# Groups of four with a wait for landing in the indirect DMAs of two routed feed-forward stages (eight-stage transformer block kernel, one core)

## Chip, core and metric

One core of a Trainium2 chip runs the whole program in one launch. The metric is the device time of that launch in microseconds (us); lower is better. Engines are called by their names in the profile: PE (TensorE), DVE (VectorE), ACT (ScalarE), POOL (GpSimd) and SP (the engine that issues the plain DMAs; SPq is its queue).

## What is computed

The reference adds eight residual blocks to x (4 sequences of 512 tokens, 128 features): an attention-like mixing block and a feed-forward block in turn, four times. The change touches the feed-forward blocks of the kernel's stages "1" and "3", in which each token goes to 2 of 8 experts (stage 1) or to 1 of 8 (stage 3):

```python
# stage 1 (L0_ffn), on the layer norm of x
global_idx, weights = _route(tokens, uzman_embeddings, onbellek_durumu)   # 2 of 8 experts, softmax weights
h = gelu(einsum('nd,edh->enh', tokens, W1) + b1[:, None, :])               # 128 -> 512
out_all = einsum('enh,ehd->end', h, W2) + b2[:, None, :]                   # 512 -> 128
out = sum(weights[..., None] * out_all[global_idx, arange(N)[:, None]], axis=1)
# stage 3 (L1_ffn), on the layer norm of x
one_hot = one_hot(argmax(xf @ Wg + bg, axis=-1), e)
h = gelu(einsum('td,edh->eth', xf, W1), approximate=True)
out = einsum('etd,te->td', einsum('eth,ehd->etd', h, W2), one_hot)
...
x = x + _L0_ffn_ref(_layernorm(x)); x = x + _L1_xcond_ref(...); x = x + _L1_ffn_ref(_layernorm(x)); ...
```

## The kernel before

Two streams of work, c0 and c1, each carry two of the four sequences (1024 tokens) through stages 1 to 5; their instructions share all engines. Stage 6 follows behind a barrier, with all four sequences apart.

A routed stage (generator `routed`, lines 1053 to 1187) does the following for each stream. The gates choose experts, and `rank` (DVE, L2811 at its end) gives each token a slot in a table in DRAM, in which every block of 128 rows belongs to one expert: 23 blocks in stage 1, 15 in stage 3. POOL then scatters the normed tokens to their slots in `zslots`, one indirect DMA of 128 rows of 512 bytes each (`zs`, L3059): 16 of them per stream in stage 1 (8 tiles of tokens times 2 experts), 8 in stage 3. When all have landed, SP fetches four blocks at a time back (`zl`, L1585). PE transposes them (`zbt`, L1827) and multiplies each block by its expert's first weights (`re1`, L1836; DVE copies these weights to a fixed place, L2781), ACT applies the gelu (L2311 in stage 1, L2308 in stage 3), and PE multiplies by the second weights (`re2`, L1846). DVE copies the result out of PSUM (L2820), and SP stores four blocks at a time in `yslots` (`ysd`, L1590). When all of them are stored, POOL gathers each token's rows back (`yg`, L3065), again 16 DMAs per stream in stage 1 and 8 in stage 3, and DVE adds them to x (`ya`, L2832 in stage 1, L2827 in stage 3), one half of the stream's tokens (k = 0, 1) at a time. In stage 1, small products with the experts' second bias run beside the scatter (`br1`: PE L1858, ACT L2295; `br2`: PE L1867, DVE L2675).

Every engine runs its own list of instructions in order. What stands where in these lists is decided when the program is built: the streams are generators that ask a planner (`Plan.merge`) for time on a chain of engines, with an estimated cost in us for each step, and the planner gives the next place to the stream whose step it expects to start first, with biases and a random term from a table per stage (`ORDER`). An expected cost therefore also sets the order on all engines. The planner counts 1.27 us for each indirect DMA on POOL (engine "G").

PE's completion is signalled by one semaphore (`T`, s_pe0 in the order rows), DVE's, ACT's and POOL's likewise; a DMA adds 16 to a semaphore of its own when it has landed, for instance `zs0` for the scatters of c0, `yg0_0` and `yg0_1` for the two halves of its gathers. `D(name).now()` is the value that such a semaphore has when everything that was issued on it up to this place has landed. In the trace's rows, a wait whose end the profile lays to nobody is called "remote".

Of the kernel before, what the change touches and what calls it, by code (L numbers as in the profile page):

```python
# [210 lines left out]
class Plan:  # L211
# [24 lines left out]
    def emit(self, *step):  # L236
        self.order.append(step)
# [92 lines left out]
def build(nc, d, out):  # L330
    ctx = ExitStack()
    with ctx:
        def sb(name, shape, dt=F32):
            return ctx.enter_context(nc.sbuf_tensor(name, shape, dt))[tuple(slice(None) for _ in shape)]


        T, A, V, G = (Sem(nc, ctx, n) for n in ("pe", "act", "dve", "pool"))
        chan = {}

        def D(name):  # L340
            if name not in chan:
                chan[name] = Sem(nc, ctx, name, 16)
            return chan[name]
# [53 lines left out]
        for i in range(2):  # L397
# [3 lines left out]
            n = f"c{i}"  # L401
            m = sb(n + "m", [128, 6144])
# [52 lines left out]
        for c in cos:  # L455
# [8 lines left out]
            for name, top, nk in (("1", 2, 23), ("3", 1, 15)):  # L464
                r = Co()
# [76 lines left out]
        for e in six:  # L542
            f, o = Co(), [4960 * (e.i // 2)]
# [67 lines left out]
        def uid():  # L611
            ids[0] += 1
            return ids[0]
# [34 lines left out]
        def do(name, *args, chain, after):  # L648
            _, t = yield Want(chain, after=after)
            emit(name, *args)  # L650
            return t[-1]
# [177 lines left out]
        def chain(c):  # L829

            for name, run in (("1", lambda: routed(c, "1")), ("2", lambda: both(stage2, c)),
                              ("3", lambda: routed(c, "3")), ("4", lambda: both(stage4, c)),
                              ("5", lambda: ahead(stage5, experts5, c))):
                while name == "2" and len(zero) < 5:
# [218 lines left out]
        def routed(c, name):  # L1053

            r, n = c.route[name], uid()
# [4 lines left out]
            def add(k, t):  # L1060
                yield from do("ya", r, n, k, chain=[("V", .7 if name == "3" else 2.4)], after=t)
                added.append(k)
# [54 lines left out]
            def scatter():  # L1117
                t = tp
                for j in range(8):
                    for m in range(r.top):  # L1120
                        t = yield from do("zs", r, n, j, m, chain=[("G", 1.27)], after=t)
                slots.append(t + 2.0)

            def fetch():
                while not slots:
                    yield
                for h in range(nb):
# [7 lines left out]
                    have[h] = zt, t[1]  # L1135

            plan.spawn(scatter(), c)
            plan.spawn(weights(), c)
            plan.spawn(fetch(), c)
# [7 lines left out]
            for i in range(nk + 1):  # L1147
# [12 lines left out]
                if i >= 1:  # L1160
                    k = i - 1
# [8 lines left out]
                    else:  # L1170
                        _, t = yield Want([("T", .95)], [], th)
# [8 lines left out]
            t = max(stored)  # L1180
            for k in range(2):
                for j in range(4):
                    for m in range(r.top):
                        t = yield from do("yg", r, n, 4 * k + j, m, chain=[("G", 1.27)], after=t)
                plan.spawn(add(k, t + 2.0), c)
            while len(added) < 2:
                yield
# [1862 lines left out]
        def gpsimd(e):  # L3050
            w = Waits(e)
# [4 lines left out]
            def zs(r, n, j, m):  # L3056
                w.wait_ge(*D("st_z").at("z"))
                w.wait_ge(*V.at(("pos", n)))
                e.indirect_dma_start(out=r.ZD, out_offset=bass.IndirectOffsetOnAxis(ap=r.pos[m][:, j:j + 1], axis=0), in_=r.Z[:, j, :],  # L3059
                                     in_offset=None).then_inc(*D(f"zs{r.i}")(("zs", n)))  # L3060

            def yg(r, n, j, m):
                for q in range(2):
                    w.wait_ge(*D(f"ys{r.i}_{q}").at(("ys", n)))
                e.indirect_dma_start(out=r.G[m][:, j, :], out_offset=None, in_=r.YD,  # L3065
                                     in_offset=bass.IndirectOffsetOnAxis(ap=r.pos[m][:, j:j + 1], axis=0)
                                     ).then_inc(*D(f"yg{r.i}_{j // 4}")(("yg", n, j // 4)))
# [84 lines left out]
            def ybg(c, m, vec):  # L3152
                w.wait_ge(*G.now())
                e.tensor_tensor(c.y, c.y, bc4(vec), ALU.add).then_inc(*G(("yb", m)))

            run(dict(zs=zs, yg=yg, fence=fence, pre=pre, ln=ln, cx0=cx0, pre2=pre2, lnb=lnb, s0base=s0base, en=en, s1g=s1g, sa=sa, bar=bar,
                     lng=lng, rp=rp, rps=rps, ybg=ybg))

# [187 lines left out]
```

## Time and profile before

| | us |
|---|---|
| runs of before (device time) | 4064.53, 4055.73, 6461.04; median 4064.53 |
| the profiled execution's own time | 4054.01 |
| span of that execution (first to last instruction) | 4052.2 |
| PE busy in the span | 3451.3 (85%) |
| DVE, ACT, POOL busy | 2498.2 (62%), 2258.0 (56%), 1420.3 (35%) |
| mean granted TensorE clock, share of full | 0.939 |
| indirect DMAs on POOL, stages 1 and 3 | 48 scatters (L3059), 48 gathers (L3065) |

All numbers of the trace are from one profiled execution, and times within it count from its first instruction. Stage 1 lies at about 200 to 440 us, stage 2 up to about 1060, stage 3 at about 1033 to 1173, and stages 4 and 5 follow up to about 2115, where the barrier before stage 6 stands. In a timeline row, the bracket at the end is the time that the engine sat idle before the row and who ended that wait.

### The profile page before, as it was taken

How to read it: one execution, taken by the hardware profiler on the slowest of the kernel's cores; microseconds unless marked ns; L12 is line 12 of the kernel's file. 1: busy time of each engine (PE TensorE's matmuls, PEld its weight loads, DVE VectorE, ACT ScalarE, POOL GpSimd, SP SyncE). 2: the span in 40 equal slices, each digit the busy share in tenths (PEclk: the TensorE clock that was granted, in tenths of full speed). 3: DMA queues.
4: the chain of work that ended last, by engine and by line, in shares of the span. 5: the costliest groups of instructions: out<-in, count | busy, mean ns of one | idle time of the engine just before them, and what ended most of it. 6: DMA issues, size and time to landing. Idle time of an engine off the chain costs nothing.

```text
span 4052.2 us, 56657 instructions
## 1 busy us (share of the span) xinstructions
PE 3451.3 (85%) x21861; PEld 1520.2 (38%) x21861; DVE 2498.2 (62%) x4786; ACT 2258.0 (56%) x3258; POOL 1420.3 (35%) x1419
## 2 busy tenths in 40 slices
PE   5637799899789988998886888999999999988987
PEld 3437333333543344334552233333333333333334
DVE  6642543543455435543658878778777778777754
ACT  4514455455245464545322766767777777667773
POOL 4541443443344402440004144343442433433321
PEclk8758899999899999999996999999999999999987
DMA  3011100000210010001112001111111110110100
GB/s 121 10 53 55 57 17 12 17 17 12 74 55 17 22 38 12 16 22 57 33 29 57 25 25 49 44 33 41 44 46 27 44 49 25 50 42 25 42 12 16
DMA packets 139215, 146.07 MB, mean 36 GB/s; under 512 B 37241, under 2 KB 120649, under 8 KB 137238
## 3 DMA queue, kind: packets, MB, share of 16 engines
q1 hardware_dynamic: 135876, 136.16, 11.5%
q0 software_dynamic: 3072, 6.30, 0.5%
q8 instruction: 174, 2.85, 0.3%
q14 instruction: 93, 0.76, 0.1%
HBM read 69.20 MB, written 12.59 MB: 20 GB/s over the span
## 4 chain that ended last, share of the span: by engine, by line
PE 57%; DVE 23%; ACT 9%; POOL 5%; issue 3%; another core or an unknown queue 2%; DMA 1%; SPq 1%; POOLq 0%; DVEq 0%; ACTq 0%
PE ps L1978 7%; PE ps L1962 6%; PE ps L2173 5%; DVE c1sm L2950 4%; DVE c0sm L2950 4%; PE ps L2090 3%; PE ps L2159 3%; ACT wA L2422 2%; PE ps L1903 2%; PE ps L2010 2%; PE ps L2117 2%; PE ps L2217 2%; PE ps L2209 2%; PE ps L1836 2%; POOL c1m L3131 2%
## 5 line engine op out<-in xcount | busy, mean ns | idle before, releaser
L2422 ACT ACTIVATE wA<-ps 128x1024 f32<-128x1024 f32 (+1 forms) x576 | 580.3, 1022 | 190.2 <-PE ps L2159 185.8
L2950 DVE TENSOR_REDUCE c1sm<-ps 128x2 f32<-128x1024 f32 x384 | 454.7, 1219 | 103.8 <-PE ps L2117 102.2
L2950 DVE TENSOR_REDUCE c0sm<-ps 128x2 f32<-128x1024 f32 x384 | 453.6, 1219 | 92.0 <-PE ps L2117 90.4
L2725 DVE TENSOR_REDUCE c1sm<-ps 128x2 f32<-128x1024 f32 x128 | 154.8, 1222 | 194.0 <-PE ps L1927 191.8
L2725 DVE TENSOR_REDUCE c0sm<-ps 128x2 f32<-128x1024 f32 x128 | 154.5, 1222 | 168.3 <-PE ps L1927 165.8
L2422 ACT ACTIVATE c0m<-ps 128x1024 f32<-128x1024 f32 (+1 forms) x195 | 199.4, 1023 | 63.4 <-PE ps L2159 62.0
L2422 ACT ACTIVATE wB<-ps 128x1024 f32<-128x1024 f32 (+1 forms) x189 | 193.1, 1022 | 56.8 <-PE ps L2159 55.4
L3080 POOL TENSOR_SCALAR c1sm<-c1sm 128x4 f32<-128x4 f32 x40 | 7.9, 196 | 536.0 <-DVE c1sm L2494 535.8
L2159 PE MATMUL ps<-c0ar 64*128 64x512 bf16 (+1 forms) x864 | 165.3, 385 | 28.1 <-DVE c1sm L2950 12.1
L1962 PE MATMUL ps<-c0ar 64*128 64x512 f32 (+1 forms) x640 | 178.3, 635 | 11.4 <-ACT c0ar L2345 7.4
L3080 POOL TENSOR_SCALAR c0sm<-c0sm 128x4 f32<-128x4 f32 x40 | 7.9, 196 | 512.6 <-DVE c0sm L2494 427.2
L2173 PE MATMUL ps<-wA,c1m 128*9 128x512 f32 (+1 forms) x932 | 182.1, 599 | 1.5 <-ACT wB L2422 0.9
L2159 PE MATMUL ps<-c1ar 64*128 64x512 bf16 (+1 forms) x864 | 163.9, 387 | 21.3 <-DVE c0sm L2950 11.8
L3124 POOL TENSOR_TENSOR c0ar<-c0ar 128x1024 f32<-128x1024 f32 x52 | 123.0, 2366 | 165.2 <-ACT c0ar L2352 132.0
L1962 PE MATMUL ps<-c1ar 64*128 64x512 f32 (+1 forms) x640 | 174.2, 621 | 5.1 <-ACT c1ar L2345 2.7
L2117 PE MATMUL ps<-c1ar 62*128 62x512 bf16 x768 | 151.1, 392 | 23.0 <-DVE c1sm L2950 6.9
L2117 PE MATMUL ps<-c0ar 62*128 62x512 bf16 x768 | 149.5, 390 | 17.8 <-DVE c0sm L2950 9.0
L3137 POOL TENSOR_TENSOR c0m<-c0m 128x512 f32<-128x512 f32 (+1 forms) x78 | 96.7, 1240 | 183.8 <-DVE c0m L2939 162.1
L3124 POOL TENSOR_TENSOR c1ar<-c1ar 128x1024 f32<-128x1024 f32 x52 | 123.6, 2377 | 104.9 <-ACT c1ar L2352 91.4
L2352 ACT ACTIVATE c0ar<-ps 128x1024 f32<-128x1024 f32 (+1 forms) x96 | 98.3, 1024 | 108.6 <-PE ps L1965 108.2
L2352 ACT ACTIVATE c1ar<-ps 128x1024 f32<-128x1024 f32 (+1 forms) x96 | 98.3, 1024 | 108.5 <-PE ps L1965 106.9
L2939 DVE TENSOR_TENSOR c0m<-ps,CST 128x1024 f32<-128x1024 f32 x72 | 88.2, 1225 | 61.0 <-PE ps L2090 60.9
(979 smaller groups left out, 8290.2 us busy)
## 6 DMA issues: line engine op xcount, KB each, us to landing
c0ar<-c0m SPq DMA_DIRECT2D x216, 128.0 KB, 2.4
c1ar<-c0m SPq DMA_DIRECT2D x216, 128.0 KB, 2.4
c0m<-rscr SPq DMA_DIRECT2D x96, 128.0 KB, 3.0
c1m<-rscr SPq DMA_DIRECT2D x96, 128.0 KB
wA<-in_x SPq DMA_DIRECT2D x1, 4112.0 KB, 21.9
wA<-in_x SPq DMA_DIRECT2D x1, 4096.0 KB, 13.0
wA<-in_lay SPq DMA_DIRECT2D x3, 1346.0 KB, 5.9
wB<-in_lay SPq DMA_DIRECT2D x3, 1346.0 KB, 5.9
```

What stands on the lines that cost most here:

```text
L1962: e.matmul(j4(u.ap, h, 512)[0:n, :], c.KT[s][r, o:o + n], c.QT[s][r, :], start=True, stop=False)
L1978: x = e.matmul(acc.ap[64 - 64 * h:128 - 64 * h, :], c.VV[g % 2][0:n, i, 64 * h:64 * h + 64], P.ap[0:n, h, :], start=first, stop=end, skip_ ...
L2090: i = e.matmul(U.ap[:, 512 * k:512 * k + ncol], j4(ww, k), src, start=True, stop=True)
L2117: i = e.matmul(j4(u.ap, p, 512), c.QS[r, s, 128 * j:128 * j + 128], c.KS[r, s, :], start=True, stop=True)
L2159: i = e.matmul(j4(u.ap, p, 512)[0:n, :], K, c.QS[r, s, :], start=True, stop=True)
L2173: x = e.matmul(acc.ap[32 * i:32 * i + (9 if g % 2 else 18), :], vv, Ps[i // 2].ap[0:n, i % 2, :], start=first, stop=end, skip_group_check= ...
L2352: e.activation(P.ap[0:n, :, :], u.ap[0:n, :].rearrange("p (h q) -> p h q", h=2), ACT.Exp, scale=0.125).then_inc(*A(("P", n0, g, i), free=[u]))
L2422: e.activation(P.ap[0:n, :, :], u.ap[0:n, :].rearrange("p (a q) -> p a q", a=2), ACT.Exp, scale=S8).then_inc(*A(("P8", n0, s, k), free=[u]))
L2725: e.tensor_reduce(c.sm[:, 2 * (g % 2), 2 * j:2 * j + 2], u.ap.rearrange("p (h k) -> p h k", h=2)[:, :, 0:n], AX, ALU.max, negate=True).the ...
L2950: e.tensor_reduce(c.mneg[:, j, :, s // 4, s % 4], u.ap.rearrange("p (a k) -> p a k", a=2), AX, ALU.max, negate=True).then_inc(*V(free=[u]))
L3124: e.tensor_tensor(S.ap, P0.ap if P0 else S.ap, P.ap, ALU.add).then_inc(*G(("S", n0, g), free=[P0, P] if P0 else [P]))
L3137: e.tensor_tensor(o[:, 0:ncol], o[:, 0:ncol], o[:, 512:512 + ncol], ALU.add).then_inc(*G(("rp", n)))
```

## The change

POOL waits, before every fourth indirect DMA after the first of a stream's scatter or gather, until those issued before on the same semaphore have landed. That makes 3 waits for each run of 16 and 1 for each run of 8: 12 in stage 1 and 4 in stage 3. The planner's expected cost of the waiting DMA rises from 1.27 to 3.47 us, so that the order on all engines is planned anew from that place to the barrier before stage 6.

```diff
@@ routed, scatter() @@
                     for m in range(r.top):
-                        t = yield from do("zs", r, n, j, m, chain=[("G", 1.27)], after=t)
+                        rest = 2.2 if (r.top * j + m) % 4 == 0 and (j or m) else 0.0
+                        t = yield from do("zs", r, n, j, m, chain=[("G", 1.27 + rest)], after=t)
@@ routed, the gathers @@
                     for m in range(r.top):
-                        t = yield from do("yg", r, n, 4 * k + j, m, chain=[("G", 1.27)], after=t)
+                        rest = 2.2 if (r.top * j + m) % 4 == 0 and (k or j or m) else 0.0
+                        t = yield from do("yg", r, n, 4 * k + j, m, chain=[("G", 1.27 + rest)], after=t)
@@ gpsimd @@
             def zs(r, n, j, m):
                 w.wait_ge(*D("st_z").at("z"))
                 w.wait_ge(*V.at(("pos", n)))
+                if (r.top * j + m) % 4 == 0 and (j or m):
+                    w.wait_ge(*D(f"zs{r.i}").now())
                 e.indirect_dma_start(out=r.ZD, ...)
             def yg(r, n, j, m):
                 for q in range(2):
                     w.wait_ge(*D(f"ys{r.i}_{q}").at(("ys", n)))
+                if (r.top * j + m) % 4 == 0 and (j or m):
+                    w.wait_ge(*D(f"yg{r.i}_{(r.top * j + m - 1) // r.top // 4}").now())
                 e.indirect_dma_start(out=r.G[m][:, j, :], ...)
```

On POOL, at the scatters of stage 1, the list before was this (zslots is the table in DRAM, c0ar and c1ar hold the normed tokens; s_zs00 is the semaphore on which the scatters of c0 land):

```order
L3059 DMA zslots<-c0ar 2944x128 [waits s_dve0,s_st_z0]
L3059 DMA zslots<-c0ar 2944x128 x15
L3059 DMA zslots<-c1ar 2944x128 [waits s_dve0]
L3059 DMA zslots<-c1ar 2944x128 x15
L3065 DMA c0ar<-yslots,c0ar 128x128 [waits s_ys0_10,s_ys0_00]
```

and it is now this, with the lines shifted by the added ones:

```order
L3063 DMA zslots<-c0ar 2944x128 [waits s_dve0,s_st_z0]
L3063 DMA zslots<-c0ar 2944x128 x3
L3063 DMA zslots<-c0ar 2944x128 [waits s_zs00]
L3063 DMA zslots<-c0ar 2944x128 x3
L3063 DMA zslots<-c0ar 2944x128 [waits s_zs00]
L3063 DMA zslots<-c0ar 2944x128 x3
L3063 DMA zslots<-c0ar 2944x128 [waits s_zs00]
L3063 DMA zslots<-c0ar 2944x128 x3
L3063 DMA zslots<-c1ar 2944x128 [waits s_dve0]
L3063 DMA zslots<-c1ar 2944x128 x3
L3063 DMA zslots<-c1ar 2944x128 [waits s_zs10]
L3063 DMA zslots<-c1ar 2944x128 x3
```

The scatters of c1 still stand behind all of those of c0; nothing else has come between them. On SP, the DMAs after these scatters were (zl fetches from zslots, ysd stores to yslots):

```order
L1585 DMA c0ar<-zslots 128x4x128 [waits s_zs00]
L1585 DMA c0ar<-zslots 128x4x128
L1585 DMA c0ar<-zslots 128x4x128 [waits s_pe0]
L1590 DMA yslots<-c0m 128x4x128 [waits s_dve0]
L1585 DMA c0ar<-zslots 128x4x128 [waits s_pe0]
L1585 DMA c1ar<-zslots 128x4x128 [waits s_zs10]
L1585 DMA c0ar<-zslots 128x4x128 [waits s_pe0]
```

and are now

```order
L1587 DMA c0ar<-zslots 128x4x128 [waits s_zs00]
L1587 DMA c0ar<-zslots 128x4x128
L1587 DMA c0ar<-zslots 128x4x128 [waits s_pe0] x2
L1592 DMA yslots<-c0m 128x4x128 [waits s_dve0]
L1587 DMA c0ar<-zslots 128x4x128 [waits s_pe0]
L1592 DMA yslots<-c0m 128x4x128 [waits s_dve0]
L1587 DMA c1ar<-zslots 128x4x128 [waits s_zs10]
```

The first fetch of c1 has moved behind the fifth fetch and the second store of c0, and PE's first transposes and experts of c1 have moved behind more experts of c0 with it. The third place is POOL's list at the gathers of c1 in stage 1; before it was

```order
L3080 TENSOR_SCALAR c0ve<-c0mv 128x4 [waits s_pool0,s_dve0]
L3082 TENSOR_TENSOR c0rs<-c0ve,MH 128x4 [waits s_pool0]
L3080 TENSOR_SCALAR c0ve<-c0mv 128x4 [waits s_pool0,s_dve0]
L3082 TENSOR_TENSOR c0rs<-c0ve,MH 128x4 [waits s_pool0]
L3065 DMA c1ar<-yslots,c1ar 128x128 [waits s_ys1_10,s_ys1_00]
L3065 DMA c1ar<-yslots,c1ar 128x128 x15
L3124 TENSOR_TENSOR c0ar<-c0m 128x1024 [waits s_pool0,s_act0]
```

and now it is

```order
L3086 TENSOR_SCALAR c0ve<-c0mv 128x4 [waits s_pool0,s_dve0]
L3088 TENSOR_TENSOR c0rs<-c0ve,MH 128x4 [waits s_pool0]
L3071 DMA c1ar<-yslots,c1ar 128x128 [waits s_ys1_10,s_ys1_00]
L3086 TENSOR_SCALAR c0ve<-c0mv 128x4 [waits s_pool0,s_dve0]
L3088 TENSOR_TENSOR c0rs<-c0ve,MH 128x4 [waits s_pool0]
L3071 DMA c1ar<-yslots,c1ar 128x128 x3
L3071 DMA c1ar<-yslots,c1ar 128x128 [waits s_yg1_00]
```

The second layer norm of c0 in stage 2 (TENSOR_SCALAR and TENSOR_TENSOR on c0ve and c0rs) now stands behind the first gather of c1, and with it behind the stores of c1's last experts.

## Rows read from the trace of the kernel before

**Rows 1.** Stretches: its length, each engine's busy us (instructions), PE clock, DMA share, GB/s.

```profile
core 0: us, PE busy (x) PEld busy (x) DVE busy (x) ACT busy (x) POOL busy (x), PEclk, DMA share, GB/s
240.00:500.00 260.00, 169.91 (x1148) 129.20 (x1148) 94.85 (x228) 97.21 (x263) 86.59 (x80) 0.80 0.18 56
500.00:1040.00 540.00, 522.88 (x2955) 204.02 (x2953) 245.42 (x366) 271.22 (x437) 214.62 (x99) 0.99 0.06 16
1040.00:1200.00 160.00, 115.50 (x785) 87.69 (x784) 71.14 (x188) 50.13 (x79) 54.34 (x50) 0.86 0.22 74
```

**Rows 2.** Timeline of POOL, stage 1 scatters: start, length, operation, [idle before and its end].

```profile
238.01 1.24 POOL L3059 DMA_INDIRECT zslots<-c0ar  x1 [11.69 <-DVE c1ar L2616]
...
257.41 1.03 POOL L3059 DMA_INDIRECT zslots<-c0ar  x1 [0.30 <-issue]
258.75 1.16 POOL L3059 DMA_INDIRECT zslots<-c1ar  x1 [0.30 <-issue]
...
277.92 0.96 POOL L3059 DMA_INDIRECT zslots<-c1ar  x1 [0.30 <-issue]
```

**Rows 3.** Timeline of the other engines beside the scatters of c1, stage 1.

```profile
259.73 28.39 SPq L1585 DMA_DIRECT2D c0ar<-zslots  x3
...
259.98 2.07 PE L1867 MATMUL ps<-EQS,c1m 8*128 8x128 f32 x8 [2.73 <-issue]
...
261.98 1.01 PE L1858 MATMUL ps<-CST,c1ar 128*8 128x128 f32 x4
279.64 0.69 DVE L2675 TENSOR_TENSOR X<-X,ps 128x512 f32<-128x512 f32 x1 [20.57 <-remote]
283.16 0.59 ACT L2295 ACTIVATE c1m<-ps 8x512 f32<-8x512 f32 x1 [23.23 <-remote]
...
283.80 2.07 PE L1867 MATMUL ps<-EQS,c1m 8*128 8x128 f32 x8 [20.80 <-ACT c1m L2295]
...
286.62 1.11 PE L1827 MATMUL ps<-CST,c0ar 128*128 128x128 f32 x4 [0.76 <-issue]
```

**Rows 4.** Timeline beside the gathers of c0 (POOL from 364.04), stage 1.

```profile
372.53 1.14 ACT L2311 ACTIVATE c1m<-ps,c1ar 128x128 f32<-128x128 f32 x4 [5.32 <-remote]
...
375.69 1.91 PE L1836 MATMUL ps<-c1m,c1ar 128*128 128x128 f32 x8
...
382.87 0.94 POOL L3065 DMA_INDIRECT c0ar<-yslots,c0ar  x1 [0.30 <-issue]
...
386.65 2.18 ACT L2311 ACTIVATE c1m<-ps,c1ar 128x128 f32<-128x128 f32 x8 [12.07 <-remote]
387.95 2.07 PE L1846 MATMUL ps<-wA,c1m 128*128 x8 [10.34 <-ACT c1m L2311]
```

**Rows 5.** Timeline at the last gather of c1 in stage 1 and beside it.

```profile
427.26 0.31 PE L1939 MATMUL ps<-c0ar 64*128 64x77 bf16 x8 [1.52 <-issue]
...
433.69 0.95 POOL L3065 DMA_INDIRECT c1ar<-yslots,c1ar  x1 [0.31 <-issue]
...
436.56 0.81 DVE L2732 TENSOR_REDUCE ps<-ps 128x8 f32<-128x616 f32 x1 [5.69 <-remote]
```

**Rows 6.** Timeline behind the scatters of c0 in stage 3: fetch and first transpose.

```profile
1057.58 4.56 SPq L1585 DMA_DIRECT2D c0ar<-zslots  x3
1060.68 1.06 PE L1827 MATMUL ps<-CST,c0ar 128*128 128x128 f32 x4
```

**Rows 7.** Timeline at the scatters of c1 in stage 3 and beside them.

```profile
1080.14 1.06 POOL L3059 DMA_INDIRECT zslots<-c1ar  x1 [14.26 <-DVE c1ar L2811]
...
1089.65 0.96 POOL L3059 DMA_INDIRECT zslots<-c1ar  x1 [0.30 <-issue]
1091.58 1.09 ACT L2308 ACTIVATE c0m<-ps 128x512 f32<-128x512 f32 x2 [5.86 <-remote]
1091.90 0.36 SPq L1585 DMA_DIRECT2D c1ar<-zslots  x1
...
1092.34 1.32 PE L1846 MATMUL ps<-wA,c0m 128*128 x8 [4.39 <-ACT c0m L2308]
```

## The prediction, made before the change was run

> **What bounds the kernel now.** I read the page's busy times first, then the stretches by time, then the timelines of POOL and of the others around every indirect DMA, since the change touches only these. Over the span PE is busy 85% of the time, so the kernel is mostly PE-bound: from 500 to 1040 us PE works 522.9 of 540 us at clock 0.99 [rows 1]. A delay before such a stretch, or one saved, passes on nearly whole to the end. The routed stages are the exception: from 240 to 500 us PE works only 169.9 of 260 us, at a mean clock of 0.80, and from 1040 to 1200 only 115.5 of 160 [rows 1]. Some 90 us and 45 us of idle PE lie there, and the indirect DMAs stand in the middle of both.
>
> Now the timeline of POOL. In stage 1, the 16 scatters of c0 start at 238.01 and the last at 257.41, one every (257.41 - 238.01) / 15 = 1.29 us; those of c1 follow without a gap until 277.92 [rows 2]. SP, which waits for the landing of all of c0's, issues its first fetch at 259.73 [rows 3], 2.32 us after the last of them started. In stage 3 the same distance is 1091.90 - 1089.65 = 2.25 us [rows 7].
>
> The reader should next look at who stands still beside it. PE does two small products of the bias terms (L1867 at 259.98, done at 262.05, and L1858 at 261.98, done at 262.99). DVE needs the first and starts at 279.64; ACT needs the second and starts at 283.16; both waits are called "remote" [rows 3]. Nothing else that they wait for is open. So PE's signals arrive about 17.6 and 20.2 us late. PE itself has the transposes of c0 behind a product that needs ACT's answer, so it idles 20.8 us, and the first transpose of c0's fetched tokens comes at 286.62 although SP had ordered them at 259.73 [rows 3]. The same picture comes with every long run of indirect DMAs, and nowhere else. Beside the gathers of c0, ACT waits 5.3 and 12.1 us for "remote", and PE idles 10.3 us [rows 4]. Beside those of c1, DVE takes at 436.56 what PE had finished at 427.57, 9.0 us later [rows 5]. Beside the 8 scatters of c1 in stage 3, ACT waits 5.9 us and PE 4.4 [rows 7].
>
> When do the late signals come through? About when the last DMA in flight lands: the last issues are at 277.92, 382.87, 433.69 and 1089.65, plus 2.3 us gives 280.2, 385.2, 436.0 and 1092.0, against 279.64, 386.65, 436.56 and 1091.58 [rows 2 to 5, 7]. ACT's 283.16 is 3 us later than that. I read from this that PE's semaphore signals are held back while indirect DMAs follow each other without a pause, and are let go once they have landed. That is a reading of five places, not something a row says.
>
> **The change, part by part.** *The waits themselves.* The fifth DMA of a run now starts when the fourth has landed, 2.32 us after its start, and not 1.29 us after it: 1.03 us more, with some start-up behind the wait, so I take 1.2 us. 16 waits cost POOL 19 us. A run of 16 is 3.6 us longer, a run of 8 1.2 us. The bounds are 1.0 us (row) and 2.3 us, if the whole landing came on top of the pitch.
>
> *The hold on PE's signals* is what each wait may end. A group of four takes 3 x 1.29 + 2.4 = 6.3 us. Eight scatters in a row cost PE 4.4 us in stage 3 [rows 7], so I count 2.2 us of PE's time for each group of four beside busy experts. The bounds are 0 (four are too few to hold anything) and 4 us (the signals of most of a group come only with its landing).
>
> *Start of c0's experts in stage 1.* The scatter of c0 lands at 259.7 + 3.6 = 263.3. From fetch to first transpose stage 3 takes 1060.68 - 1057.58 = 3.1 us [rows 6], so PE can start at 266.4 where it started at 286.6: 20.2 us saved, if the bias products' signals come within a group. But now the scatters of c1 (262 to 285, landed at 287.4) run beside c0's experts: 4 groups x 2.2 = 8.8 us back. Net -11.4 us. That c1's tokens land 7.2 us later costs nothing: 8 blocks of c0 stand before its first fetch in the new order, and two stores of c0 do.
>
> *Gathers of c0, stage 1.* The two waits of ACT are 17.4 us [rows 4]; less 8.8 for four groups, -8.6 us. The 3.6 us that POOL takes longer are covered by c1's experts.
>
> *Gathers of c1, stage 1.* -9.0 us of delay in c0's attention [rows 5], +4.4 for two groups in its way, so -4.6 us. The gathers end 3.6 us later and so does c1's entry into stage 2; PE has c0 alone meanwhile: between 0 and 3.6 us, I take 2.
>
> *Stage 3.* Two groups of 2.2 us are what the 8 scatters cost now, so nothing is saved; c0's scatter lands 1.2 us later with PE waiting for it. +1.2 us.
>
> *The new order.* It differs in small exchanges of neighbours from the scatters to the barrier before stage 6. What was good for late signals need not be good now; I have no row for its worth and take 0, with 10 us to both sides. The one that I can name is the layer norm of c0 behind the first gather of c1: it waits for c1's last stores. If both streams keep their distance, this costs next to nothing.
>
> Sum: -11.4 - 8.6 - 4.6 + 2 + 1.2 = -21.4 us. The profiled execution took 4054.0 us (span 4052.2 and 1.8 around it), so 4032.6; I say **4033 us**. The median of the shown runs is 4064.5, 10.5 above the profiled one, but one of its three is the outlier 6461; 4055.7 is closer, so I leave the sum at the profile's level and widen the upper end.
>
> A rule of the skill speaks against the change. [Rows 2, 3] show that a scatter has landed 2.3 us after its start while the next starts after 1.3, so landings overlap with issues. The Trainium skill ("DMA: Bandwidth & Descriptors", rules for kernel authors) says to issue a DMA early, do other work, and wait late, so that the fixed cost overlaps; its section on the anatomy of a DMA puts this fixed cost at about 2.0 us, mostly the receipt of the write. An estimate by that page is 16 x 2.0 = 32 us lost and nothing won. The rows agree with its latency; they show beside it the late signals of PE, of which the page says nothing.
>
> **Rivals.** (1) *Full relief.* Four DMAs hold nothing back. For it: PE's work in the first microseconds of a run shows no "remote" wait; in stage 3 the late one comes near the end of eight. Then -20.2 - 17.4 - 9.0 - 4.4 + 2 + 1.2 = -47.8, 4006 us.
>
> (2) *The waits are pure cost*, slower than before. Place: POOL's pause after each fourth DMA. If the signals need longer than the pause to get through, as ACT's of 283.16 did (3 us after the landing), or if something other than the DMAs holds them, PE stays blocked through all groups, and each wait moves the end: 16 x 1.2 = +19 us, 4073. It decides once a held signal needs more than about 1 us of silence. Against it: in four of five places the signal came within 1.5 us of the landing.
>
> (3) *The whole landing is added each time*, 16 x 2.3 = +37 us, 4091, with nothing won. This is the forecast of the rule above at the row's price. Against it: the pitch of 1.29 us that the wait replaces is in that time.
>
> (4) *The order eats the gain.* Experts of c0 alone for longer, with c1's later, leave PE waiting for gelu and weight copies. For it: ORDER's numbers and the order go together, and PE's list changed in many places. Against: the pieces are small. About 4054 us.
>
> That the waits do nothing can be excluded: landing takes 2.3 us, the pitch is 1.3.
>
> **How the numbers follow.** Forecast (between -10 and -35 us) 0.45; full relief 0.2; order, no change 0.15; pure cost 0.15; whole landing 0.05. A range from 3998 to 4076 us takes in (1), (4) and (2) and leaves out (3) and what is better than full relief. The likeliest case alone is 4019 to 4046. 2% of the time, about what a measurement of this kernel can tell from no change, is 81 us; none of the cases reaches that, the best gives 48 and the worst 37. I leave 0.03 for faster and 0.03 for slower by more, and 0.94 for within 2%.
>
> **What would show it.** In the profile after: POOL's runs with pauses of 1.3 to 1.6 us before every fifth DMA; the first transpose of c0 at about 266, not 286; waits for "remote" that are shorter than 4 us; PE busy in 240 to 500 us by some 20 us more, at a higher clock. The forecast is wrong if ACT L2295 and DVE L2675 still wait until c1's scatters have all landed (then rival 2), if no "remote" wait is left (rival 1), or if these are short and the span is unchanged (rival 4).

## The result: 36 us faster where the kernel before takes 4058 us, 19 us slower where it takes 3996

In the runs that were made for the comparison, the changed kernel took 4022.21 us (median of 5 runs, 4017.17 to 4030.49) and the kernel before 4058.25 (five runs, one of them the outlier of 6461.04). The ratio, taken without the outlier, is 0.9914, 95% interval 0.9895 to 0.9934: faster by 0.9% (36 us by these medians, 35 without the outlier), within 2% as forecast, and within the predicted range of 3998 to 4076 around 4033.

The experiments then showed something that this ratio hides. The kernel before, without a character changed, runs at one of two levels, and every group of runs (the runs made together on one chip) stayed at its level: about 4058 us here (the **upper level**), 3996 us in five of six later groups (the **lower level**). The changed kernel takes 4022 us beside the upper level and 4014 beside the lower one. There it is slower than the kernel before, by 0.48% (1.0048, interval 1.0034 to 1.0062).

The profile after, taken beside the upper level, in the same stretches as [rows 1] (length, busy us of PE, PEld, DVE, ACT and POOL, PE clock, DMA share, GB/s):

```profile
240.00:500.00 260.00, 205.35 (x1354) 141.09 (x1356) 108.97 (x240) 114.80 (x294) 100.05 (x85) 0.88 0.19 58
500.00:1040.00 540.00, 504.33 (x2830) 200.49 (x2826) 246.23 (x406) 256.16 (x410) 210.83 (x105) 0.97 0.07 22
1040.00:1200.00 160.00, 132.37 (x850) 86.68 (x851) 79.07 (x147) 66.34 (x101) 60.49 (x45) 0.93 0.17 53
```

From 240 to 500 us PE works 35.4 us more than in [rows 1], at a granted clock of 0.88 instead of 0.80. That is where the time came from. In the second stretch PE works less than before, because the program is earlier and another part of it lies there.

The same kernel's timeline at the scatters of c0 and at the first fetched tokens of c0, against [rows 2, 3] (start, length, engine, line, operation, tiles, and in brackets the idle time and its end):

```profile
240.35 0.96 POOL L3063 DMA_INDIRECT zslots<-c0ar  x1 [0.30 <-issue]
...
242.85 0.96 POOL L3063 DMA_INDIRECT zslots<-c0ar  x1 [1.54 <-DMA zslots<-c0ar]
...
251.88 2.07 PE L1869 MATMUL ps<-EQS,c1m 8*128 8x128 f32 x8 [0.68 <-issue]
253.99 0.69 DVE L2677 TENSOR_TENSOR X<-X,ps 128x512 f32<-128x512 f32 x1 [2.87 <-issue]
...
256.38 1.02 PE L1860 MATMUL ps<-CST,c1sm 128*8 128x128 f32 x4 [2.43 <-DVE c1sm L2672]
...
257.44 0.59 ACT L2297 ACTIVATE c1m<-ps 8x512 f32<-8x512 f32 x1 [5.61 <-PE ps L1860]
...
261.69 7.01 SPq L1587 DMA_DIRECT2D c0ar<-zslots  x4
...
264.50 1.11 PE L1829 MATMUL ps<-CST,c0ar 128*128 128x128 f32 x4 [4.35 <-DMA c0ar<-zslots]
```

POOL's pause is 1.54 us where the issue alone leaves 0.30, so a wait takes 1.24 us of POOL. The two signals that were held longest in [rows 3] now come at once: DVE gets PE's bias product 0.04 us after its end (251.88 + 2.07 = 253.95) and not 17.6, and ACT gets the other one 0.04 us after its end (257.40) and not 20.2. The first transpose of c0's fetched tokens is at 264.5, not 286.6.

The hold is not gone, only shorter. The changed kernel has a trace at each level, with the same instructions in the same order, so what a wait needed at the lower level tells what it needed at the upper. At the scatters of c1 in stage 3, ACT needs the product of L1838 (its 1.06 us run to 1048.85 and 1041.02). At the upper level ACT starts 2.3 us after its end:

```profile
1047.79 1.06 PE L1838 MATMUL ps<-c0m,c0ar 128*128 128x128 f32 x8
...
1051.16 0.60 ACT L2310 ACTIVATE c0m<-ps 128x512 f32<-128x512 f32 x1 [3.47 <-PE ps L1848]
```

and at the lower level 0.04 us after it:

```profile
1039.96 1.06 PE L1838 MATMUL ps<-c0m,c0ar 128*128 128x128 f32 x8
...
1041.06 0.60 ACT L2310 ACTIVATE c0m<-ps 128x512 f32<-128x512 f32 x1 [1.19 <-PE ps L1838]
```

Compared in this way over the whole span, the kernel before has 13 waits for PE that end more than 0.3 us late at the upper level, 85 us in all and up to 20.2 each; the changed kernel has 9, 16 us in all and up to 2.5 each. All 22 end beside a run of indirect DMAs or within 5.3 us of the start of its last one. Eight of the nine end 1.8 to 2.1 us after the start of a group's last DMA, in the pause that the change makes or behind the last group. The label misleads here: no wait from 200 to 1220 us of the changed kernel is called "remote", while [rows 3 to 5, 7] hold six of them.

### The profile page after: what moved, and what is told of

Its sections match the earlier page's. It is cut to its first block, busy times and chain, and to the rows that moved or that the text cites. A ratio compares the mean times of both kernels' runs of the same rounds, so it can differ in the third digit from the quotient of the medians.

```text
span 4020.7 us, 56655 instructions
## 1 busy us (share of the span) xinstructions
PE 3462.3 (86%) x21861; PEld 1523.6 (38%) x21861; DVE 2504.5 (62%) x4786; ACT 2260.0 (56%) x3258; POOL 1421.5 (35%) x1419
## 4 chain that ended last, share of the span: by engine, by line
PE 58%; DVE 23%; ACT 8%; POOL 5%; issue 4%; DMA 1%; SPq 1%; POOLq 0%; DVEq 0%; ACTq 0%
PE ps L1980 7%; PE ps L1964 7%; PE ps L2175 5%; DVE c1sm L2952 4%; DVE c0sm L2952 4%; PE ps L2092 3%; PE ps L2161 3%; ACT wA L2424 2%; PE ps L1905 2%; PE ps L2012 2%; PE ps L2119 2%; PE ps L2219 2%; PE ps L2211 2%; PE ps L1848 2%; PE ps L1838 2%
## 5 line engine op out<-in xcount | busy, mean ns | idle before, releaser
L2952 DVE TENSOR_REDUCE c1sm<-ps 128x2 f32<-128x1024 f32 x384 | 454.8, 1220 | 103.1 <-PE ps L2119 101.7
L2952 DVE TENSOR_REDUCE c0sm<-ps 128x2 f32<-128x1024 f32 x384 | 453.6, 1220 | 92.1 <-PE ps L2119 90.5
## 6 DMA issues: line engine op xcount, KB each, us to landing
wA<-in_x SPq DMA_DIRECT2D x1, 4096.0 KB, 12.8
```

What stands on the lines that cost most here:

```text
L2952: e.tensor_reduce(c.mneg[:, j, :, s // 4, s % 4], u.ap.rearrange("p (a k) -> p a k", a=2), AX, ALU.max, negate=True).then_inc(*V(free=[u]))
```

## The experiments

All changes of time are against the kernel before, timed on the same chip in the same group of runs.

### First group: the two halves of the change, and its two places

*Waits alone*, the planner's numbers and so every engine's order as before:

```diff
-rest = 2.2 if (r.top * j + m) % 4 == 0 and (j or m) else 0.0         # scatters
-rest = 2.2 if (r.top * j + m) % 4 == 0 and (k or j or m) else 0.0    # gathers
+rest = 0.0
```

> POOL's 16 waits as in the change, but the planner counts 1.27 us for each indirect DMA as before, so every engine's list keeps the order of before. Theory 'held signals' (PE's signals are late while indirect DMAs follow each other without a pause; the waits let them through): most of the gain of 31 to 36 us is here, 4020 to 4032 us, and the waits for 'remote' of 20.6 and 23.2 us are gone. Rival 'order' (the gain is the new order's): 4055 to 4075 us, since 16 waits of 1.2 us are added and nothing is won.

Measured: 4004.09 us against 3995.69, ratio 1.0020 (1.0011 to 1.0029), 8.4 us slower.

*New order alone*, both waits on POOL removed from the changed kernel:

```diff
-                if (r.top * j + m) % 4 == 0 and (j or m):
-                    w.wait_ge(*D(f"zs{r.i}").now())
...
-                if (r.top * j + m) % 4 == 0 and (j or m):
-                    w.wait_ge(*D(f"yg{r.i}_{(r.top * j + m - 1) // r.top // 4}").now())
```

> The order of the change on all engines, but POOL does not wait. Theory 'held signals': 4050 to 4066 us, like before, and the long waits for 'remote' beside the scatters of c1 in stage 1 are back (15 to 20 us). Rival 'order': 4005 to 4022 us, at least as good as the change, since the pauses of POOL are spared.

Measured: 4011.59, ratio 1.0040 (1.0027 to 1.0054), 15.9 us slower.

*New order, waits in the scatters only* (the second pair of those lines removed):

> The order of the change; POOL waits in the scatters only (8 waits), not in the gathers. Theory 'held signals' with its terms as they lie in the two traces: the start of the first gather of c0 moved 20 us earlier (1.7 of it from before the scatters), so some 18 us below the kernel with the new order and no waits, and stage 3's scatters give up to 4 more; waits for 'remote' beside the gathers are back. 4030 to 4040 us. If one place gave all of the gain: 4022 here or in its counterpart.

Measured: 4016.43, ratio 1.0044 (1.0031 to 1.0058).

*New order, waits in the gathers only* (the first pair removed):

> The order of the change; POOL waits in the gathers only (8 waits). Theory 'held signals': the 20 us wait beside the scatters of c1 is back; the gathers' part, 10 to 16 us, is kept: 4040 to 4050 us. Together with the counterpart the two parts add up to the gain of the whole within 5 us if the places are independent.

Measured: 4011.44, ratio 1.0039 (1.0025 to 1.0052).

The numbers of the theory were missed in all four, because the kernel before itself took 3996 us in this group and not 4058. One number of the rival fits, 4011.59 in 4005 to 4022 for the new order alone, but by luck: it was meant as a gain and is a loss of 15.9 us. The kernel with the new order and no waits shows no "remote" wait at all, although its indirect DMAs follow each other exactly as before. So the hold on PE's signals is not something that a stream of indirect DMAs always brings. What the four do show is the price of each part where nothing is held: waits 8.4 us, order 15.9 us. On the new order the medians put the scatters' waits at 4.8 us and the gathers' at -0.2; neither is clear of the noise, since the three intervals overlap almost wholly.

### Second group: the two kernels themselves, more waits, fewer waits

*The kernel before*, unchanged:

> The kernel before, unchanged, profiled on the chip of the experiments, where it took 3996 us in the last group of runs and not 4058. Theory 'the hold is a property of the chip, not of the kernel': its trace has no wait for 'remote' beside the indirect DMAs, the first transpose of c0 comes some 20 us earlier than 286.6, and its stretch from 240 to 500 us has over 205 us of PE. Rival 'the late signals are hidden elsewhere': they are there as before, and the 60 us come from another stage.

Measured: 3994.61 us, ratio 0.9995 (0.9985 to 1.0004), the lower level again. Its timeline, to be read against [rows 3]:

```profile
256.33 0.59 ACT L2295 ACTIVATE c1m<-ps 8x512 f32<-8x512 f32 x1 [3.11 <-PE ps L1858]
256.97 2.07 PE L1867 MATMUL ps<-EQS,c1m 8*128 8x128 f32 x8 [0.68 <-ACT c1m L2295]
257.81 4.60 SPq L1585 DMA_DIRECT2D c0ar<-zslots  x3
259.08 0.69 DVE L2675 TENSOR_TENSOR X<-X,ps 128x512 f32<-128x512 f32 x1 [3.01 <-PE ps L1867]
260.90 1.12 PE L1827 MATMUL ps<-CST,c0ar 128*128 128x128 f32 x4 [1.86 <-DMA c0ar<-zslots]
```

and POOL's of the same kernel beside it:

```profile
256.82 0.96 POOL L3059 DMA_INDIRECT zslots<-c1ar  x1 [0.31 <-issue]
258.09 0.96 POOL L3059 DMA_INDIRECT zslots<-c1ar  x1 [0.30 <-issue]
259.35 0.96 POOL L3059 DMA_INDIRECT zslots<-c1ar  x1 [0.30 <-issue]
```

The pitch of the scatters is 1.27 us, much as in [rows 2] (1.28 to 1.29). But DVE starts 0.04 us after the bias product's end (256.97 + 2.07 = 259.04), and ACT 0.04 us after L1858's. The first transpose of c0 is at 260.9. In the trace's records of the 5109 signals of PE, the latest is 0.15 us behind the end of its matmul; in the profile of the kernel before at the upper level the latest is 20.1 us behind.

The profile's table of DMA issues has a plainer mark of the level. At the upper level, in the kernel before, it can give no time from issue to landing (the last number of a row) for indirect DMAs:

```profile
zslots<-c0ar POOLq DMA_INDIRECT x24
```

and at the lower level, in the same kernel, it does:

```profile
zslots<-c0ar POOLq DMA_INDIRECT x24, 2.3
```

At the lower level the trace records 16 steps of the semaphore for each of these 24 scatters, 384 in all; at the upper level it records 134. All three traces at the upper level (before, after, and the one of the third group) lack the landing time for all four kinds of indirect DMA; the eleven at the lower level lack it for two at most. Whether the missing steps came together or only their records are lost, the traces do not tell. But the missing time tells the level of a profile at a glance, that of the changed kernel too. The stretches of the kernel before at the lower level:

```profile
240.00:500.00 260.00, 215.62 (x1430) 144.05 (x1430) 113.33 (x244) 124.93 (x310) 104.69 (x86) 0.90 0.19 58
500.00:1040.00 540.00, 503.89 (x2912) 213.37 (x2911) 249.44 (x431) 253.68 (x407) 214.77 (x111) 0.97 0.08 24
1040.00:1200.00 160.00, 139.17 (x835) 79.21 (x833) 78.19 (x129) 75.53 (x114) 62.17 (x42) 0.96 0.15 46
```

PE works 45.7 us more from 240 to 500 than in [rows 1], since more of the program fits into this stretch, and 23.7 us more from 1040 to 1200. The theory "the hold is not the kernel's" stands; "they are there as before" falls. That it belongs to the chip falls later, when this same chip shows the upper level.

*The changed kernel*, unchanged:

> The changed kernel, unchanged. Theory 'the gain exists only where PE's signals are held': without the hold the pauses (8.4 us of the kernel with waits in the old order) and the new order (15.9 us of the kernel without waits) are left, 4010 to 4022 us against 3996, slower by 0.3 to 0.6%. Rival 'the change wins on any chip': 3965 us, 0.9% below before.

Measured: 4014.38, ratio 1.0048 (1.0034 to 1.0062). The theory gave 4010 to 4022; "the change wins on any chip" falls.

*Groups of two* in the old order:

```diff
-                if (r.top * j + m) % 4 == 0 and (j or m):
+                if (r.top * j + m) % 2 == 0 and (j or m):
```

> POOL waits before every second indirect DMA (40 waits for 16), in the old order. With no held signals the 16 waits cost 8.4 us, 0.53 us each: by that 3996 + 21 = 4017 us if every wait costs the same. If a chip holds signals and waits release them: below the kernel with groups of four there.

Measured: 4028.54, ratio 1.0081 (1.0067 to 1.0095), 32.7 us slower, 12 more than expected. 40 waits cost 0.82 us each, 16 cost 0.53. The stretch of this run shows where some of it lies:

```profile
240.00:500.00 260.00, 194.47 (x1278) 138.92 (x1280) 102.62 (x238) 110.89 (x289) 95.46 (x84) 0.84 0.19 58
```

and the one of the kernel with waits alone:

```profile
240.00:500.00 260.00, 208.44 (x1392) 141.53 (x1394) 111.88 (x244) 121.60 (x305) 101.15 (x84) 0.89 0.19 58
```

The first transpose of c0 is at 271.8 us, against 264.2 with groups of four; 2.8 us of that are from before the first scatter. PE waits longer for the tokens, and its mean granted clock in this stretch is 0.84 instead of 0.89. How much of the 12 us each of the two explains is not shown.

*One wait*, put into the kernel before:

```diff
+                if r.i == 1 and not (j or m):
+                    w.wait_ge(*D("zs0").now())
```

> The kernel before with a single wait: the first scatter of c1 in each routed stage waits until all of c0's have landed. Without held signals: 3996 to 3998 us (one pause of 1.2 us in stage 1, none in stage 3, where POOL is idle there anyway). Where signals are held: the signals of 262.05 and 262.99 come through within the pause or not before the end of c1's scatters; 10 to 20 us saved by the first, nothing by the second.

Measured: 3996.77, ratio 0.9998 (0.9989 to 1.0007). As expected of the lower level; it says nothing of the upper.

### Third and fourth group: which part of the new order costs

*The planner's 2.2 us at the scatters only, no waits*:

```diff
 rest = 2.2 if (r.top * j + m) % 4 == 0 and (j or m) else 0.0         # scatters, kept
-rest = 2.2 if (r.top * j + m) % 4 == 0 and (k or j or m) else 0.0    # gathers
+rest = 0.0
```

> No waits on POOL; the planner counts the 2.2 us at the scatters only, so the gathers keep their old place in POOL's list (the last gather of c1 before c0's product of L3126, not behind it). The new order without waits cost 15.9 us where no signals are held. Theory 'the last gather behind c0's product': c1 entered its second half 11 us later by it, so nearly all of the cost belongs to the gathers: 3996 to 4001 us here. Rival 'the experts' order costs': 4006 to 4012 us. On a chip that holds signals (before at 4058): between 4045 and 4066 us by the theory of held signals.

This group of runs fell on the upper level: the kernel before took 4057.98 us. Measured: 4055.16, ratio 0.9991 (0.9982 to 1.0001), the same within the measurement. It ran on the chip of the second group, where the same kernel before had taken 3996 us. The level is therefore no fixed property of a chip. The late signals are back, in POOL's timeline and that of the others:

```profile
274.48 0.96 POOL L3061 DMA_INDIRECT zslots<-c1ar  x1 [0.30 <-issue]
```

```profile
258.43 2.07 PE L1869 MATMUL ps<-EQS,c1m 8*128 8x128 f32 x8 [4.89 <-issue]
276.70 0.69 DVE L2677 TENSOR_TENSOR X<-X,ps 128x512 f32<-128x512 f32 x1 [23.25 <-issue]
...
283.73 1.11 PE L1829 MATMUL ps<-CST,c0ar 128*128 128x128 f32 x4 [0.75 <-issue]
```

The bias product ended at 260.5, and DVE took it at 276.70, 16.2 us later and 2.2 us after the start of the last scatter. That is about when this scatter lands (2.2 to 2.3 us in the profiles at the lower level), as in the five places of the prediction. This time the profile calls the wait "issue" and not "remote"; a reader who searches for one word would miss it, and should compare the end of the producer with the start of the consumer.

This run also separates the waits from the order at the upper level. Its lists and those of the changed kernel are the same on every engine until PE's matmuls at 357 us, beside the gathers of c0; up to there the two kernels, both at the upper level, differ by the waits alone. The last matmul before the first difference starts at 356.4 us in the changed kernel and at 389.3 here, 32.8 us later, although the first scatter is 1.4 us earlier here. So by then the waits have brought 34 us. This order by itself brings little: against the kernel before at the same level, c0's first gather is 4.4 us earlier, of which 3.1 are from before the first scatter.

*The planner's 2.2 us at the gathers only, no waits* (the other line kept):

> No waits on POOL; the planner counts the 2.2 us at the gathers only (the last gather of c1 stands behind c0's product of L3126). Theory 'the last gather behind c0's product': 4006 to 4012 us, as the whole new order without waits, where no signals are held. Rival 'the experts' order costs': 3996 to 4001 us. On a chip that holds signals: 4055 to 4075 us.

Measured at the lower level: 4008.19 against 3996.83, ratio 1.0034 (1.0023 to 1.0045), 11.4 us slower. The theory gave 4006 to 4012, its rival 3996 to 4001. So of the 15.9 us that the new order costs, 11.4 come with the cost number at the gathers. POOL's timeline of the kernel with the new order and no waits shows it:

```profile
388.39 0.94 POOL L3067 DMA_INDIRECT c1ar<-yslots,c1ar  x1 [0.30 <-issue]
398.49 2.36 POOL L3126 TENSOR_TENSOR c0ar<-c0m 128x1024 f32<-128x1024 f32 x1 [9.15 <-ACT c0m L2354]
401.00 0.96 POOL L3067 DMA_INDIRECT c1ar<-yslots,c1ar  x1 [0.15 <-POOL c0ar L3126]
```

The sixteenth gather of c1 stands behind a product of c0's stage 2 that waits for ACT. It starts 12.6 us after the fifteenth. In the kernel before at the same level it starts 1.25 us after it:

```profile
388.94 0.94 POOL L3065 DMA_INDIRECT c1ar<-yslots,c1ar  x1 [0.30 <-issue]
390.19 0.95 POOL L3065 DMA_INDIRECT c1ar<-yslots,c1ar  x1 [0.30 <-issue]
```

It stands there too in the kernel of this experiment (12.8 us after the fifteenth), whose planner differs from that of before by the 2.2 us at the gathers alone. But that number moves more than this gather: PE's list differs from that of before in over 90 places. That the one gather is the cause fits its 11.8 us and is not shown; it was never moved alone. The changed kernel has the same at the upper level:

```profile
404.19 0.95 POOL L3071 DMA_INDIRECT c1ar<-yslots,c1ar  x1 [0.30 <-issue]
410.33 2.35 POOL L3130 TENSOR_TENSOR c0ar<-c0m 128x1024 f32<-128x1024 f32 x1 [5.19 <-ACT c0m L2354]
412.83 0.96 POOL L3071 DMA_INDIRECT c1ar<-yslots,c1ar  x1 [0.16 <-POOL c0ar L3130]
```

The other 4.5 us, by subtraction, would be the scatters' part of the order; at the lower level it was not run alone.

### Fifth and sixth group: waits in the old order once more, and groups of eight

*The kernel with the waits alone*, a second time:

> The kernel with the 16 waits in the order of before a second time, since a session decides which of two levels the kernel before takes (3996 or 4058 us), and it has been seen only at the lower one (4004 against 3996). At the lower level: 4002 to 4007 us again. At the upper level, where PE's signals are held: theory 'the waits release the signals, the order only costs' gives 4022 - 10 = 4012 us, by the 10 us that it was below the whole change at the lower level; the rival 'under held signals the new order is what helps' gives 4040 us or more.

Measured: 4005.09 against 3996.80, ratio 1.0019 (1.0010 to 1.0028): the lower level, and the 8.3 us repeat the 8.4.

*Groups of eight* in the old order, one wait in each run of 16 (`% 8` for `% 4`):

> POOL waits once in each run of 16 (4 waits in all, none in stage 3), in the old order. At the lower level (before at 3996): 0.53 us each by groups of four, so 3998 us; 0.8 us each by groups of two would be 3999. At the upper level (before at 4058), theory of held signals: each pause lets PE's signals through once in 10 us, so more than half of the 36 us gained by the change, and the old order's 10 us on top: 4025 to 4040 us.

Measured: 3997.60 against 3995.06, ratio 1.0003 (0.9994 to 1.0012). At the lower level it costs nothing that can be measured. How much of the hold it would lift at the upper level was not seen.

### Where the time stands, by landmarks

Starts in us, from the timelines of the profiled executions; the end is the span. "First experts" is the first transpose of c0's fetched tokens, "stage 2" the first product of c0's attention (PE L1903, L1905 in the changed kernel), and stage 3 runs from its first scatter to its last gather.

| | first scatter | first experts | first gather of c0 | c0 in stage 2 | last gather of c1 | stage 3 first | stage 3 last | end |
|---|---|---|---|---|---|---|---|---|
| before, upper level | 238.0 | 286.6 | 364.0 | 418.8 | 433.7 | 1046.3 | 1170.2 | 4052.2 |
| after, upper | 236.3 | 264.5 | 343.8 | 387.4 | 412.8 | 1014.1 | 1133.9 | 4020.7 |
| before, lower | 236.0 | 260.9 | 338.6 | 375.3 | 390.2 | 994.4 | 1109.3 | 3997.5 |
| after, lower | 234.6 | 263.3 | 338.7 | 379.2 | 404.8 | 1005.6 | 1123.0 | 4017.5 |
| waits alone, lower | 235.0 | 264.2 | 341.2 | 381.4 | 400.9 | 1000.2 | 1115.8 | 4003.2 |
| scatters' order alone, upper | 234.9 | 283.7 | 359.6 | 413.9 | 428.8 | 1040.6 | 1168.4 | 4056.7 |
| order alone, lower | 234.6 | 259.7 | 335.7 | 376.1 | 401.0 | 1002.2 | 1118.2 | 4009.8 |

Between the levels, the kernel before loses 43.5 us until c0 is in stage 2, of which 2.0 are from before the first scatter and the rest beside or just behind indirect DMAs, and 54.7 us in all (62 by the medians). The changed kernel loses 8.2 us until there, and 3.2 us in all by these two profiles, 7.8 us by the medians.

## Why the prediction was right, and where it was not

The number was right: 4022 in a range of 3998 to 4076, on the side that was forecast, 36 us gained where 21 were predicted. The reason was right for the level at which it was measured and false as a statement about the kernel. That both kernels were timed at the upper level was luck: in five of the six groups that followed, the kernel before ran at the lower one, where the changed kernel loses 19 us.

- **The hold and its release: right, at the upper level.** "About when the last DMA in flight lands" held again in a kernel that the prediction had not seen (DVE at 276.70), and the signals come through groups of four: DVE gets its product after 0.04 us in place of 17.6. It is not the whole rule, though: in the trace before, 7 of the 13 late waits end in the middle of a run, such as those of ACT at 372.53 and DVE at 381.02, before the last gather at 382.87. That the waits bring the gain is shown up to c0's gathers: with the same lists, the kernel without them is 34 us behind by then. The scatters' part of the order gave 2.8 us there, no more than its interval. The waits in the old order were never run at the upper level, nor was the gathers' part of the order.
- **The wait's own cost: right on POOL, too high on the path.** 1.2 us were taken for each and 1.24 measured. Rival 2 put all 16 on the path, 19 us; the runs give 8.4.
- **"Hold per group of four" was the step that failed in size.** It took 2.2 us for each of eight groups beside busy experts, 17.6 us, from the eight scatters of stage 3. With it, c0 should have entered stage 2 20.0 us earlier (11.4 and 8.6); it entered 31.4 us earlier (418.8 to 387.4). Of these, 1.7 us are from before the scatters, which leaves 29.7. Without any hold the same two terms give 37.6. So the eight groups kept 7.9 us, POOL's pauses included, 1.0 each and not 2.2. The trace agrees roughly: ACT's late waits in these eight groups add up to 10.0 us. The whole gain of the span, 31.5 us, is there by this landmark; what comes behind it adds up to nothing.
- **"Stage 3: nothing is saved" was wrong.** It looked at c1's scatters alone. Beside the gathers of c0 in stage 3 the trace before has late signals too (ACT 2.8 and 2.4 us, DVE 4.8), and they had no term. From its first scatter to its last gather the stage is 4.2 us shorter in the changed kernel, where +1.2 was predicted. Behind it some of this is lost again, and no run shows by what.
- **"Start of c0's experts": right.** 266.4 was worked out for the first transpose, 264.5 measured, of which 1.7 us are from before the scatters.
- **"The new order ... take 0" was wrong.** It costs 15.9 us at the lower level, outside the 10 us allowed to each side. The named place, c0's layer norm behind the first gather of c1, costs little: the second one starts at 370.45 us with the new order alone and at 369.83 in the kernel before at the same level. A place that the prediction did not name is the likelier one: the sixteenth gather behind c0's product. At the upper level it is in the trace as well (412.8), so the change won there in spite of its order. What the last gather costs at that level was not measured.
- **Rivals.** By the prediction's own sign, "no 'remote' wait is left", rival 1 (full relief, 4006) would have won. The sign was a poor one: the word is gone, but nine waits of the changed kernel are still 0.7 to 2.5 us late, which is the forecast's "shorter than 4 us". That 4006 plus the order's 15.9 gives 4022 proves nothing, since the price is one of the lower level. Rival 2, pure cost, and rival 4, the order eats the gain, are both what happens at the lower level: 8.4 and 15.9 us alone, 18.6 together. Whether the two overlap is not shown; their sum, 24.3 us or 0.6%, is within the interval of the whole (0.34 to 0.62%). Rival 3 is excluded: its 37 us are over four times what the 16 waits cost at the lower level.
- **The rule "issue early, wait late".** Where no signal is held, the waits only cost, 8.4 us for 16 and 32.7 us for 40. On this side the rule of the Trainium skill ("DMA: Bandwidth & Descriptors", rules for kernel authors) is right in direction. The price is 0.5 to 0.8 us for each wait, and not the whole latency, since the pitch that it replaces is part of it (1.24 us of POOL are left) and other work hides some of the rest.

What the prediction never asked was whether what it saw was the kernel's. It had one profile and three runs, all at one level, and a wait that the profile laid to nobody. No rival said "these waits are not always there". That one would have been the answer for five of the six groups of runs that followed.

The best kernel depends on the level. At the lower level nothing beats the kernel before, and groups of eight (3997.6) or one wait (3996.8) are level with it. At the upper level the changed kernel is the best that was run. The obvious next candidate is waits in the old order, or groups of eight; both were run only at the lower level.

## What to carry to other kernels

A wait that ends long after its producer is done, whatever the profile calls it, may belong to the session and not to the kernel: profile the unchanged kernel again, in another session, before building a change on it, and time a change beside its own kernel before at each level that shows up. Where it does belong to the level, cutting a long stream of indirect DMAs by a wait for landing is a cheap insurance, about half a microsecond a wait here. And enter such a wait into a planner's costs only after looking at what it moves: the cost number cost more (15.9 us) than the waits (8.4 us), and in its order one gather had slipped behind another stream's work.

## What the runs showed of the hardware that was not expected

- The same program takes 3996 or 4058 us, 1.5% apart, for all runs of a group, and one chip showed both. At the upper level PE's completion signals arrive up to 20.2 us late beside back-to-back indirect DMAs; at the lower level at most 0.15 us late, with the same DMAs at much the same pitch (1.28 to 1.29 and 1.27 us). The upper level's trace also records only some of the steps of those DMAs' own semaphores (134 of 384 for c0's scatters), the lower level's all 384. What sets the level is open; nothing in the runs tells.
- At the upper level a late signal comes through about when the last indirect DMA in flight lands, 2.2 us after its start in the newest case, and sometimes in the middle of a run. A wait for landing at every fourth DMA (1.24 us more of pause on POOL) leaves waits that end at most 2.5 us late, against 20.2: about 1.0 us a group is left on the path, the pause included.
